# Work units of the attention loop as pairs of PSUM banks, with the scores in the same rotation

## The reference, cut to what matters

```python
qf, kf = taylor_exp(q), taylor_exp(k)     # [1, x/2, x_i x_j/(4 sqrt 2)], 16 features a head
A_qk = jnp.tril(qf @ kf^T);  y = A_qk @ v  # 16 heads, 64 values a head, 2048 tokens
y = y * rsqrt(mean(y*y) + eps) * g_weight;  attn = y @ Wo.T
h = gelu(xn @ ternary(W1).T + b1);  ffn = h @ ternary(W2).T + b2
out = x + attn + ffn                       # xn = layernorm(x), 2048 x 1024 a core
```

## Time and profile before

| | us |
|---|---|
| Median of 3 runs | 807.31 (807.04 to 869.51) |
| The profiled execution | 808.52 |
| Its span, slowest core (core 3) | 807.0 |
| Spans of the other cores | 791.4 to 802.7 |
| Mean granted PE clock of core 3 | 0.958 |
| PE busy in the span | 710.6 (88%) |

### The profile page before, as it was taken

How to read it: one execution, slowest core, us unless ns; L and a number is a source line. 1 busy time by engine, 2 the same in 40 slices (tenths; PEclk the granted TensorE clock), 3 DMA queues, 4 the chain that set the end, 5 groups by cost and what they waited for, 6 DMA issues and landing times.

```text
span 807.0 us, 11855 instructions; the slowest of 8 cores (791.4 to 807.0 us)
## 1 busy us (share of the span) xinstructions
PE 710.6 (88%) x4028; PEld 339.9 (42%) x4028; DVE 399.5 (50%) x694; ACT 287.8 (36%) x437; POOL 73.0 (9%) x111
## 2 busy tenths in 40 slices
PE   1759768877688889899999998999999999999998
PEld 1325334443444445444444443444444444444443
DVE  6769555444766666724231234453257355410564
ACT  2346537676856535424545544333300000000000
POOL 2003000101011000001111111101011000000000
PEclk9988889999699999999999998999999999999999
DMA  6997963444666621434667566444144576500675
GB/s 137 189 167 149 197 160 83 125 118 125 177 170 180 182 90 67 125 111 146 195 209 221 196 210 211 155 153 157 53 168 147 193 219 204 166 1 1 205 208 162
DMA packets 72634, 123.62 MB, mean 153 GB/s; under 512 B 34432, under 2 KB 39424, under 8 KB 72576
## 3 DMA queue, kind: packets, MB, share of 16 engines
q0 software_dynamic: 22880, 73.08, 31.6%
q1 hardware_dynamic: 49696, 49.77, 22.7%
HBM read 103.30 MB, written 16.78 MB: 149 GB/s over the span
## 4 chain that ended last, share of the span: by engine, by line
PE 70%; DMA 12%; issue 6%; ACT 5%; DVE 4%; SPq 2%; DVEq 0%; ACTq 0%; POOLq 0%
PE pW L975 7%; PE pST L1074 7%; PE pSS L1074 7%; PE pY L1074 7%; PE pW L1074 7%; PE pSS L1051 6%; PE pST L1051 6%; PE pY L1051 5%; PE pW L864 5%; PE pW L1051 5%; DMA xnT<-xn_tm 4%; PE pW L852 2%; DMA stg<-w2r 2%; ACT Am L799 2%; DMA xr<-x 2%
## 5 line engine op out<-in xcount | busy, mean ns | idle before, releaser
L778 ACT ACTIVATE stg<-stg 128x2048 f32<-128x2048 f32 x32 | 60.9, 1903 | 52.7 <-DMA stg<-w2r 52.7
L609 DVE TENSOR_SCALAR w1t<-stg,consts 128x2048 bf16<-128x2048 f32 (+1 forms) x18 | 21.1, 1174 | 111.7 <-DMA stg<-w1r 91.7
L864 PE MATMUL pW<-wv_sb,xnT 128*128 128x512 bf16 x256 | 69.2, 419 | 2.3 <-issue 2.3
L1074 PE MATMUL pST<-w2t,hT 128*128 128x512 bf16 x256 | 66.0, 379 | 0.1
L1074 PE MATMUL pW<-w2t,hT 128*128 128x512 bf16 x256 | 66.0, 379 | 0.0
L1074 PE MATMUL pSS<-w2t,hT 128*128 128x512 bf16 x256 | 66.0, 379 | 0.0
L1074 PE MATMUL pY<-w2t,hT 128*128 128x512 bf16 x256 | 66.0, 379 | 0.0
L975 PE MATMUL pW<-wo_sb,yT 128*128 128x512 bf16 x256 | 59.8, 388 | 5.7 <-ACT qf L760 4.7
L1051 PE MATMUL pSS<-xnT,w1t 128*128 128x512 bf16 x272 | 61.5, 379 | 1.8 <-ACT hT L831 1.8
L1051 PE MATMUL pST<-xnT,w1t 128*128 128x512 bf16 x272 | 61.5, 379 | 0.0
L1051 PE MATMUL pY<-xnT,w1t 128*128 128x512 bf16 x240 | 56.4, 390 | 0.4 <-DVE consts L595 0.4
(11 more groups left out here) (141 smaller groups left out, 992.6 us busy)
## 6 DMA issues: line engine op xcount, KB each, us to landing
stg<-w1r POOLq DMA_DIRECT2D x32, 1024.0 KB, 6.6
stg<-w2r POOLq DMA_DIRECT2D x32, 1024.0 KB, 6.4
xr<-x SPq DMA_DIRECT2D x16, 512.0 KB, 7.6
res_scr<-rst SPq DMA_DIRECT2D x16, 512.0 KB, 2.9
res<-res_scr SPq DMA_DIRECT2D x32, 256.0 KB, 4.3
xs<-x SPq DMA_DIRECT2D x32, 256.0 KB, 4.6
out<-osb SPq DMA_DIRECT2D x32, 256.0 KB, 3.0
wv_sb<-wv POOLq DMA_DIRECT2D x2, 1024.0 KB, 12.5
```

The lines of the kernel that those rows point to most:

```text
L609: e.tensor_single_scalar(dst, src, cc(col + 1), ALU.is_lt).then_inc(sTA, 1)
L778: e.activation(buf, buf, AF.Abs, accum_out=cc(col)).then_inc(done, 1)
L864: mm = e.matmul(work_bank(u), xnT[:, c, kd, :], wv[:, hf, kd, :], start=(kd == 0), stop=(kd == KD - 1))
L1074: return e.matmul(out_bank(n), hT[:, j, 128 * t:128 * t + 128], w2t[8 * dh + j // 4][:, j % 4, :], start=(j == 0), stop=(j == NJ - 1))
```

## The change

1. A work unit is now a pair of banks, and pSS and pW alternate over all units, scores included: bank_free(key) waits until the last unit on the same pair has been emptied. v and kx of a chunk are one unit (vk, one ACT copy of 1024 columns), qfa and qfb are one (q2, one Square of 1024), wo0 and wo1 are one (wo, one DVE copy of 1024), q and k of a block are one (qk, one DVE copy of 1024). Two early value projections make one unit (vv), a third stands alone (v1), the fourth shares one with the small query features (qv).
2. The small query features are made once a block: one matmul of 512 columns (L1 has 64 rows of output), two Squares of 32x512 on ACT, and the copy of raw q into qf1 is two DMAs of SP (q_raw) where it was a DVE copy in each iteration. The state mask m1 gets a group axis.
3. The order on PE is scores, y_before, own(i+1), update, spread_q, the output projection, the side unit, y_within. On ACT st0 comes ahead of the query features, and ysq last. On DVE the sum of squares comes after the states, the wo copy, the qk copy and the sum of |W1|. st0, st1 and ysq have one buffer.
4. The sums of |W1| of tiles 0 to 6 go to DVE (tensor_reduce with absolute value, iterations 9 to 15), those of tiles 7 to 15 stay with ACT (iterations 16 to 24).
5. Features that nobody reads (of chunks 15 and 31 for keys, 0 and 16 for queries) are left out.
6. Start: the tables are built ahead of the first tile; POOL's memsets wait for them and its load of Wqk comes after x tiles 0 to 2; the first half of Wv is two loads; tile 4 is normalised in iteration 0 and not ahead of the loop, and iterations 0 to 2 take two tiles each, the second at the iteration's end; the second half of Wv waits for tile 7 where it waited for tile 5.

```diff
-def early_v(i):
-    return i + 12 if 4 <= i < 16 else None
+def own_unit(n):
+    if 16 <= n < 28:
+        return ("kx", n)
+    return ("v", n) if n % 16 == 15 else ("vk", n)
+def side_unit(i):
+    B, ph = i // 4, i % 4
+    if i < 16:
+        base = 16 + 4 * (B - 1)
+        if ph == 2:
+            return ("qk", B + 1)
+        if ph == 3:
+            return ("qv" if B else "qg", B + 1)
+        if B:
+            return (("vv", base), ("v1", base + 2))[ph]
+    elif B < 7 and ph in (1, 2):
+        return (("qk", "qg")[ph - 1], B + 1)
+    return None
...
-    def work_bank(u):
-        return pW[:, 512 * (u % 2):512 * (u % 2) + 512]
+    def bank(key, half=0):
+        t = (pSS, pW)[PAIR_NO[UID[key]]]
+        return t[:, 512 * half:512 * half + 512]
+    def bank_free(e, key):
+        m = LAST_ON_PAIR[UID[key]]
+        if m is not None:
+            unit_emptied(e, UNITS[m])
...
     def ln_tiles(i):
-        if i <= 1:
-            return (5 + 2 * i, 6 + 2 * i)
+        if i <= 2:
+            return (4 + 2 * i, 5 + 2 * i)
...
+        def q_raw(B):
+            q_ready(e, B)
+            for g in range(2):
+                e.dma_start(out=qf1[64:128, B % 2, g, :],
+                            in_=qkT[64 * g:64 * g + 64, B % 2, 0, :]).then_inc(dQR, 16)
...
-        e.wait_ge(sXN, 6)
+        e.wait_ge(sXN, 8)
         e.dma_start(out=wv[:, 1, :, :],
...
+        def abs_sum(key, col):
+            load_done(e, key)
+            e.tensor_reduce(cc(col), stg[:, STG[LID[key]], :], AX, ALU.add,
+                            apply_absolute_value=True).then_inc(sA1D, 1)
...
         for i in range(NI):
             more = i + 1 < NI
             scores(i)
-            if i % 4 == 3 and i // 4 < 7:
-                proj_qk("k", i // 4 + 1)
-            if more:
-                if has_v(i + 1):
-                    proj_v(i + 1)
-                spread_k(i + 1)
+            if i == 0:
+                own(0)
+                own(1)
+                e.wait_ge(sSU, N_SETUP)
             y_before(i)
-            if more:
-                spread_q(i + 1, 0)
-            if early_v(i) is not None:
-                proj_v(early_v(i))
-            y_within(i)
-            if more:
-                spread_q(i + 1, 1)
+            if more and i:
+                own(i + 1)
             if i % 16 < 15:
                 update(i)
-            if more:
-                spread_q1(i + 1)
-            if i % 4 == 2 and i // 4 < 7:
-                proj_qk("q", i // 4 + 1)
+            if (i + 1) % 16 and more:
+                spread_q(i + 1)
+            if i >= 18:
+                proj_out(i - 2)
+            if side_unit(i) is not None:
+                side(side_unit(i))
...
-            if i >= 18:
-                proj_out(i - 2, 0)
-                proj_out(i - 2, 1)
+            y_within(i)
```

More of the change, by code:

```diff
@@ L651, in vec_stream @@
                             ALU.mult).then_inc(dMK, 1)
[L652 to L654 removed]
+            if i == 0:
+                features_k(0)
+            for t in ln_tiles(i)[:1]:
                 ln_a(t)
@@ new lines, in first, with side @@
+        def first(kind, o):
+            key = (kind, 0)
+            if kind == "q":
+                e.wait_ge(dQK[0], 16)
+                for t in range(4):
+                    turned(e, t)
+            proj_q_or_k(bank(key), 0, o).then_inc(pWU, 1)
+        def side(key):
+            kind, n = key
+            bank_free(e, key)
+            if kind == "qk":
+                if n == 4:
+                    e.wait_ge(dQK[1], 16)
+                for t in range(4 * (n % 4), 4 * (n % 4) + 4):
+                    turned(e, t)
+                proj_q_or_k(bank(key, 0), n, 0)
+                mm = proj_q_or_k(bank(key, 1), n, 128)
+            elif kind == "vv":
+                proj_v(bank(key, 0), n)
+                mm = proj_v(bank(key, 1), n + 1)
+            elif kind == "v1":
+                mm = proj_v(bank(key), n)
+            else:
+                q_ready(e, n)
+                mm = e.matmul(bank(key)[0:64, :], L1[:].rearrange("p h i -> p (h i)"),
+                              qkT[:, n % 2, 0, :], start=True, stop=True)
+                if kind == "qv":
+                    mm = proj_v(bank(key, 1), side_value(n))
@@ L932, in y_before @@
             for g in range(2):
-                e.matmul(yb[:, 256 * g:256 * g + 256], qf1[:, b, g, :],
-                         st1[:, b, g, :], start=False, stop=False,
+                e.matmul(yb[:, 256 * g:256 * g + 256],
+                         qf1[:, B % 2, g, 128 * c4:128 * c4 + 128],
+                         st1[:, g, :], start=False, stop=False,
                          skip_group_check=True)
@@ L937, in y_before @@
                 e.matmul(yb[:, E * h:E * h + E], qf0[:, b, h, :],
-                         st0[:, b, E * h:E * h + E], start=False, stop=False,
+                         st0[:, E * h:E * h + E], start=False, stop=False,
                          skip_group_check=True)
```

572 lines of the change are left out of this document (284 added, 288 removed).

## The result

| | before | after |
|---|---|---|
| Median | 807.77 us (12 runs) | 798.79 us (794.95 to 804.62, 12 runs) |
| Span of the slowest core, profiled | 807.0 | 803.1 (core 5) |
| Median span of the eight cores | 799.0 | 789.8 |
| PE busy, slowest core | 710.6 (88%) | 692.5 (86%) |

The ratio is 0.9894, with an interval of 0.9861 to 0.9928: some 9 us faster, within the 2%. The forecast was 760, its range began at 742 and ended at 788. PE has 18 us less to do, and gives back most of them as waits.

A forecast was written before the change was run, and what follows sets the result against it. It took a chain of DMA transposes early, then alternating PE work and a stop per iteration, as the bound. Savings of 56.3 us, 47.6 after clock and restart allowances, from 808.5 gave 760.9, forecast 760; range 742 to 788.

The forecast's parts named there:

- (c): Rival, whole kernel: dearer handoffs, and tiles 9, 10 and 11 each take 21.2 us in the pile; 805 us, chance 0.08.
- Small edits: Small features and raw q copies, each block: PE saving hidden, DMAs some 1.2 us later in SP's queue; 0 us saved.
- I take scores(7) at 106.: Start and iterations 0 to 6: scores of iteration 7 come 4 us earlier, bounds 14 earlier and 5 later.
- rule of turns between queues: Transposes in the pile: by the rule they keep a share; against it, tile 11's 21.2 us says the share is small.
- Wv's second half behind tile 7 costs qk(1) 6 to 12 us: Head: tile 7's transpose meets Wv's second half, which waits for that tile; 6 to 12 us more.
- Iterations 8 to 14, 51.3: Loop stretch with side units vv, v1, qk and qv: falls from 70.1 to 51.3 us.
- rival (b): Handoffs cost more: four restarts of 0.25 us in each of 21 iterations; 781 us, chance 0.21.
- Iteration 15, 5.5: Iteration 15 falls from 7.9 to 5.5 us, having no query features or update.
- 16 and 17 stay: Iterations 16 and 17: ACT's 5.8 us plus 0.3 of ring is the 6.1 they take now; 0 saved.
- 18 to 24, 52.2: Loop stretch: seven iterations of 6.4 us and two qk units of 3.5; 52.2 us against 69.7.
- 25 to 31, 54.0: Last loop stretch: one qk, four own values, a last iteration of 4.8; 54.0 us against 65.1.
- The clock: From iteration 8 on: granted clock costs 17 us in sum before; a third, 5.5 us, was kept as allowance.

The follow-up runs named there:

- a_pool: The changed kernel with POOL's share of the q copies of blocks 3 to 6 queued one W1 load earlier: 789.57 us, ratio 0.9788.
- c_hold: a_both, with POOL's W1 load behind the q copies of blocks 3 to 6 held until those copies have landed: 785.00 us, ratio 0.9757.
- a_both: The changed kernel with POOL's q copies one W1 load earlier and SP's of block 1 ahead of iteration 2's second transpose: 791.19 us, ratio 0.9779.
- c_spread: c_hold with Wo in four 1 MB loads ahead of W1 tiles 2, 4, 5 and 6, out of the pile: 778.32 us, ratio 0.9658.
- c_wv: a_both with the second half of Wv loaded after tile 5, as in the kernel before: 790.79 us, ratio 0.9818.
- d_all: c_spread, output projection copied in halves, third W1 load of the ternary pass held until transposes of y of chunks 30 and 31 landed: 774.64 us.
- e_w1late: d_all with ACT's sums of |W1| one iteration later, in 17 to 25: 772.28 us, ratio 0.9575.
- e_wo: e_w1late with Wo's four pieces ahead of W1 tiles 2, 3, 4 and 5: 767.04 us, ratio 0.9521.
- c_yw: a_both with y_within ahead of the output projection again from iteration 18 on, as in the kernel before: 788.93 us, ratio 0.9797.

## Why the prediction was wrong

It was 39 us too low. The nearest rival is (c), 805 with a chance of 0.08: handoffs that cost more and transposes that stand in the pile were both there in part, but neither it nor another rival had the copies of q. By its own steps:

- **Small edits, "so nothing".** This step failed. It priced the copies of raw q by what their issue costs SP (1.2 us), took the others to land as before, and never asked when any of them land past the loads that change 4 re-times. They land 10.0 us after the issue, behind a load, and scores wait 32.6 us for them on core 5. Giving them their places is worth 9 us (a_pool), and keeping loads off them perhaps a few more (c_hold: 785, not clear of a_both's noise).
- **"I take scores(7) at 106."** It came at 117.2 on the slowest core and at 112.7 in the median, beyond the bound of 5 later. That the scores start at 26 was right, and the pile started at 69 (I had 62 to 68). The step took it that a 21.2 us transpose in the pile could be had once; the pile takes its whole length of whichever small transfer stands in it, 18.48 of q, or 27.30 of xn in a_both. Spreading Wo gave 11.3 (c_spread), but gave the kernel before 12.6 too. The case that the prediction set against the Trainium skill's rule of turns between queues (DMA: Bandwidth & Descriptors, Queues, rings and completion order) is the nearer one: a transpose of 27.30 us had at most a small share of the pile. Which queue got which packet no run shows. That Wv's second half behind tile 7 costs qk(1) 6 to 12 us is not borne out either: c_wv moves it and gains nothing.
- **Iterations 8 to 14, 51.3.** The term was mis-sized. It was 66.1, of it 6.81 the wait of chunk 12; with the queues in order 58.5. Each side unit waits 0.46 to 0.77 for the copy of vk, for which I had 0.25 and a restart of 0.1; and iterations 8 and 12 take 10.0 where I had 7.9. The timeline of d_all shows why: three operations of ACT for qv stand ahead of the square of the scores and of what y_before needs (PE idle 1.46). Dearer handoffs are rival (b), in this stage; no run removes them.
- **Iteration 15, 5.5, and "16 and 17 stay".** 15 took 12.1 by the cuts of the sum, of it 6.91 the wait for q; the remaining 5.2 are as forecast, so it is again the step above that failed. 16 and 17 took 12.9 against 12.2, near what was said, and with a projection (3.5) in 17 that the sum had put elsewhere (next item). By the start of the scores 16 and 17 take 11.4 in e_w1late and e_wo, against 12.3 before (medians), with that projection in them.
- **18 to 24, 52.2.** Nearly right in the number: 55.5, and 54.1 to 54.2 in c_hold and c_spread. That is in part luck. The sum counts two projections of q and k here; side_unit() puts them in 17, 21 and 25, so there is one, and the terms without the other give 48.7. And the working wasn't right: "the wait for the mask is now covered by wo" doesn't explain the period, since c_yw takes the cover away and keeps 6.8 in iterations 20 and 24. That a ring through ACT and the pairs sets the period (6.8 in iteration 20, I had 6.4) is what fits the runs; none tests it. What in the pairing makes 18 to 24 some 14 us shorter than before (68.8 to 54.2 by the start of the scores, c_hold) was not separated.
- **25 to 31, 54.0.** The term was mis-sized: 66.6. Of the 12.6 us, 7.3 lie in iteration 31, 12.1 from its scores to up(0) where the sum had 4.8: the last transpose, behind a load, wasn't in the sum (a wait of 4.50, then 6.25 for an output projection that takes 3.61 at full clock); d_all takes most of it away. Iteration 26 takes 8.8 for 6.4, as PE waits 1.32 for DVE's copy before the small matmul of the threshold. From 27 on own and wo share a pair, and 1.24 and 1.02 of copies stand in line with PE: up to 8.9 us where the sum had 8.1 (6.4 + 1.73). Halving one copy gives back 0.5 each.
- **The clock.** 5.5 us were kept for it from iteration 8 on; the first view gives 10.0 (0.05 of 66.1, 0.10 of 12.1, 0.17 of 12.9, 0.05 of 66.6), and the head is at 0.81. The low clocks stand where the new waits are.
- **The start.** The tables ahead of the first tile cost nothing. POOL's memsets waited until 4.24 and ended at 8.28, before the first xn at 9.39, so the case of the Trainium skill's rule on two-port DVE operations (SBUF — State Buffer, SBUF: two separate sides) didn't arise for it. The ident operation, with no memset beside it now, takes 0.23 (2.93 in the earlier trace rows), as the rule has it.

```profile
1.53 0.23 DVE L532 TENSOR_SCALAR ident<-tio 128x128 bf16<-128x128 f32 x1
4.24 0.10 POOL L456 MEMSET m<- 128x8 f32 x1 [2.65 <-DVE KX L553]
9.39 0.81 DVE L521 TENSOR_SCALAR xn_tm<-xr,consts 128x1024 bf16<-128x1024 f32 x1
```

The forecast of 2.3 us for a sum of |W1| on DVE, which wasn't in the trace, was right (2.28), and the MLP stretch is unchanged as forecast: from up(0) on it is 459.0 before and 460.6 after in the medians, with 457 to 465 over the cores of both. The -3.2 of the column 31-end is the output projection of chunk 29 (3.46), which the kernel before has behind that y_within.

What stays open: the 7 us of handoffs in 8 to 14, what of the pairing gives the gain in 18 to 24, and what the change is worth with Wo spread and no other repair.

## What to carry to other kernels

A loop made shorter runs into its own transfers: for each small DMA that the next block needs, write down when it is issued, what stands ahead of it in every queue and when it lands, at the new period and not the old. When the last waiter of a chain is only 0.2 us behind another, removing it is worth 0.2 us; look for the second chain before the edit. A hold that protects the small copies makes the load behind them late, so look for who waits for that load. And a gain in a shared stretch (the pile of loads) is to be tried in the kernel before as well, or it is put down to the wrong change.

## What was unexpected of the hardware

- Eight copies of q and two of raw q are in place 5.3 us after POOL's first issue when no load is beside them (c_hold) and 10.0 us after it behind one load of 1 MB (the change).
- A single DMA transpose of a tile of xn (128x1024) took 27.30 us in the pile. One of y (128x512) took 4.61 in iteration 31 of d_all, with the load held, and 7.01 in d_half and 8.19 in the change, behind a load of 1 MB.
- DVE's copy of 1024 columns takes 1.23 to 1.24, two of 512 take 0.69 each: pairing saves DVE 0.15 in all, and makes the pair wait 0.55 longer than halves do.
